# Batch 0's first product taken by halves of the contraction depth, with eight PSUM banks open at once

## The reference

```
y    = einsum('bsi,boi->bso', x, weight[ids])
base = einsum('bth,oh->bto', y, W_up)
z    = einsum('nh,erh->ner', y, lora_A);  logits = y @ gate_w.T + bias
out  = x + base + one_hot(argmax(logits)) applied to einsum('ner,ehr->neh', z, lora_B)
```

## Time and profile before

| | |
|---|---|
| median of 3 runs | 369.82 us (369.79 to 369.99) |
| the profiled execution's own time | 369.84 us |
| its span, first to last instruction | 368.1 us |
| busy: PE / PEld / DVE / ACT | 363.1 / 325.2 / 271.6 / 157.9 us |

### The profile page before, as it was taken

One profiled execution on the slowest core, in us unless ns is written; L12 is line 12 of the kernel. 1 busy time (PEld: TensorE's weight loads), 2 busy tenths in 40 slices (PEclk: granted clock), 3 DMA queues, 4 the chain that ended last, 5 costly groups with the idle time before them and its releaser, 6 DMA issues.

```text
span 368.1 us, 5953 instructions
## 1 busy us (share of the span) xinstructions
PE 363.1 (99%) x2193; PEld 325.2 (88%) x2193; DVE 271.6 (74%) x537; ACT 157.9 (43%) x315; POOL 1.8 (0%) x11
## 2 busy tenths in 40 slices
PE   7999999999999999999999999999999999999996
PEld 5888988899888998889988898888988899888995
DVE  4777847799478999678856788567984778856773
ACT  5677724645137533456025551155413553144300
POOL 0010000000000000000000000000000000000000
PEclk9999999999999999999999999999999999999999
DMA  7999984971079620686026750476404862160003
GB/s 246 396 401 307 405 318 174 325 251 51 0 274 330 223 89 2 250 319 232 0 116 234 267 187 2 170 264 211 157 0 180 325 213 85 49 238 0 3 0 114
DMA packets 20252, 68.16 MB, mean 185 GB/s; under 512 B 2304, under 2 KB 2688, under 8 KB 20224
## 3 DMA queue, kind: packets, MB, share of 16 engines
q1 hardware_dynamic: 19936, 66.74, 50.1%
q10 hardware_dynamic: 288, 1.05, 0.8%
HBM read 59.39 MB, written 8.39 MB: 184 GB/s over the span
## 4 chain that ended last, share of the span: by engine, by line
PE 99%; DVE 0%; issue 0%
PE ps_y L787 32%; PE ps_y L790 16%; PE ps_u L798 13%; PE ps_v L798 8%; PE ps_p L798 5%; PE ps_u L806 3%; PE ps_u L808 3%; PE ps_u L804 3%; PE ps_p L804 2%; PE ps_p L806 2%; PE ps_p L808 2%; PE ps_y L768 2%; PE ps_v L804 2%; PE ps_v L808 1%; PE ps_v L806 1%; PE ps_u L880 1%
## 5 line engine op out<-in xcount | busy, mean ns | idle before, releaser
L787 PE MATMUL ps_y<-x_hilo,w_hi 128*128 128x512 f32 x512 | 161.0, 396 | 0.0
L790 PEld LDWEIGHTS ps_y<-x_hilo,w_lo 128*128 128x128 f32 x512 | 96.2, 188 | 22.7
L790 PE MATMUL ps_y<-x_hilo,w_lo 128*128 128x256 f32 x512 | 100.6, 278 | 0.0
L506 DVE TENSOR_TENSOR w_lo<-w_raw,w_hi 128x512 fp32r<-128x512 f32 x126 | 81.6, 691 | 13.6 <-ACT w_hi L370 12.9
L787 PEld LDWEIGHTS ps_y<-x_hilo,w_hi 128*128 128x128 f32 x512 | 78.5, 189 | 0.9 <-DVE w_lo L499 0.4
L370 ACT CAST w_hi<-w_raw 128x512 fp32r<-128x512 f32 x126 | 71.8, 624 | 1.7 <-DMA w_raw<-w_dram 1.6
L385 ACT COPY small<-ps_y 128x256 f32<-128x256 f32 x64 | 23.9, 373 | 104.9 <-PE ps_y L790 104.9
L557 DVE TENSOR_TENSOR y_raw<-ps_y,small 128x256 f32<-128x256 f32 x64 | 27.1, 423 | 46.3 <-ACT small L385 46.3
L798 PE MATMUL ps_u<-wide_hi,y_parts 128*128 128x256 f32 (+1 forms) x256 | 47.2, 288 | 0.0
L798 PEld LDWEIGHTS ps_u<-wide_hi,y_parts 128*128 128x128 f32 x256 | 39.4, 188 | 1.4
L393 ACT CAST zT<-ps_y 128x128 fp32r<-128x128 f32 x16 | 3.5, 270 | 75.4 <-PE ps_y L814 75.4
(11 more groups left out here) (94 smaller groups left out, 386.0 us busy)
## 6 DMA issues: line engine op xcount, KB each, us to landing
w_raw<-w_dram SPq DMA_DIRECT2D x64, 512.0 KB, 4.7
rows<-x_dram SPq DMA_DIRECT2D x16, 512.0 KB, 5.9
out_dram<-rows SPq DMA_DIRECT2D x15, 512.0 KB, 2.7
x_raw<-xT_dram SPq DMA_DIRECT2D x14, 512.0 KB, 4.9
wide_raw<-w_up_dram SPq DMA_DIRECT2D x4, 512.0 KB, 11.2
thin_raw<-w_up_dram SPq DMA_DIRECT2D x4, 512.0 KB, 12.2
wide_stage<-w_up_dram SPq DMA_DIRECT2D x4, 512.0 KB, 13.9
thin_stage<-w_up_dram SPq DMA_DIRECT2D x4, 512.0 KB, 9.4
```

What stands on the lines that cost most here:

```text
L506: dve.tensor_tensor(w_lo[:, n % RAWS, part], w_raw[:, n % RAWS, part], w_hi[:, n % RING, part].bitcast(F32), ALU.subtract).then_inc(w_read ...
L787: pe.matmul(ps_y[c % 2][:, :], w_hi[:, n % RING, i * P:(i + 1) * P], x_hilo[:, :, i, :], start=(i == 0), stop=False)
L790: last = pe.matmul(ps_y[c % 2][:, S:2 * S], w_lo[:, n % RAWS, i * P:(i + 1) * P], x_hilo[:, 0, i, :], start=False, stop=(i == KC - 1))
```

## The change

Batch 0's first product becomes `open_product`: for the first half of the depth (steps 0 to 3) all 8 blocks are started, each in a PSUM bank of its own (`ps_open`: the six banks of ps_u, ps_v, ps_p and then the two of ps_y), and then all 8 are finished with the second half (steps 4 to 7). W of batch 0 comes in half blocks of 256 KB, two blocks' halves in one transfer (`load_pair`; pairs 0 to 3 hold the first halves, 4 to 7 the second halves), in runs of 2 KB; pair 0 is two transfers of 256 KB. x[0]'s second half is issued by SP between pairs 2 and 3. The warm-up has 11 matmuls. ACT and DVE split x's first half, pairs 0 to 3, x's second half, pairs 4 and 5, unit 0, pair 6 and unit 1 before the first evacuation; pair 7 follows the evacuation of block 0, unit 2 that of block 2.

```diff
-    WARM = 18
+    WARM = 11
     def splits_at(b, c):
+        if b == 0:
+            return (OC - 1,) if c == 0 else ()
-    UNIT_AT = {(0, 5): 0, (0, 6): 1, (0, 7): 2}
+    UNIT_AT = {(0, 2): 2}
+        ps_open = [ps[:, i, :] for ps in (ps_u, ps_v, ps_p) for i in range(2)] + [ps[:, :] for ps in ps_y]
+        def y_bank(b, c):
+            return ps_open[c] if b == 0 else ps_y[c % 2]
+        def wait_for_use(engine, n):
+            if n < OC // 2:
+                engine.wait_ge(half_done, n + 1)
+            elif n < OC:
+                engine.wait_ge(block_done, 2 * (n - OC // 2) + 2)
+            else:
+                engine.wait_ge(block_done, n + 1)
+            def load_pair(n, i):
+                if n >= RAWS:
+                    wait_for_use(sp, n - RAWS)
+                h, c = n // (OC // 2), 2 * n % OC
+                depth = slice(h * HK * P, (h + 1) * HK * P)
+                if n > 0:
+                    sp.dma_start(w_raw[:, n % RAWS, :].rearrange("p (a n) -> p a n", a=2),
+                                 w[bass.ds(i * OC + c, 2), :, depth].rearrange("a p n -> p a n")
+                                 ).then_inc(w_raw_in[n % RAWS], 16)
+                else:
+                    for a in range(2):
+                        sp.dma_start(w_raw[:, 0, a * HK * P:(a + 1) * HK * P],
+                                     w[bass.ds(i * OC + a, 1), :, depth].rearrange("a p n -> (a p) n")
+                                     ).then_inc(w_half_in if a == 0 else w_raw_in[0], 16)
             i = adapter(0)
-            i = load_blocks(0, 4, i)
+            for n in range(3):
+                load_pair(n, i)
+            sp.dma_start(x_raw[:, 1, XS:KC, :], xT[0, :, XS:KC, :]).then_inc(x_raw_in[1], 16)
+            load_pair(3, i)
             for n in range(4, OC):
                 load_unit(n - 4)
-                i = load_blocks(n, n + 1, i)
+                load_pair(n, i)
...
             def y_small(b, c):
                 act.wait_ge(block_done, b * OC + c + 1)
+                if b == 0 and c >= 2:
+                    act.wait_ge(y_full_ready, c - 1)
+                act.copy(small[:, c % 2, :], y_bank(b, c)[:, S:2 * S]).then_inc(y_small_ready, 1)
...
+            def open_product():
+                for h in range(HALVES):
+                    for c in range(OC):
+                        m = h * OC + c
+                        n = m // 2
+                        for k in range(h * HK, (h + 1) * HK, 2):
+                            if c == 0:
+                                pe.wait_ge(x_ready, k // XK + 1)
+                            if m > 0:
+                                pe.wait_ge(w_ready, 2 * (m + 1))
+                            else:
+                                pe.wait_ge(w_hi_ready, k // QK + 1)
+                            at = [(c % 2 * HK + i % HK) * P for i in (k, k + 1)]
+                            for i in range(2):
+                                pe.matmul(ps_open[c], w_hi[:, n % RING, at[i]:at[i] + P], x_hilo[:, :, k + i, :],
+                                          start=(k + i == 0), stop=False)
+                            if m == 0:
+                                pe.wait_ge(w_ready, k // QK + 1)
+                            for i in range(2):
+                                last = pe.matmul(ps_open[c][:, S:2 * S], w_lo[:, n % RAWS, at[i]:at[i] + P],
+                                                 x_hilo[:, 0, k + i, :], start=False, stop=(k + i == KC - 1))
+                        if h == 1:
+                            last.then_inc(block_done, 1)
+                        elif c % 2 == 1:
+                            last.then_inc(half_done, 1)
...
                 if b == 0:
                     pe.wait_ge(gl_ready, 2)
+                    pe.wait_ge(y_full_ready, 6)
```

More of the change, by code:

```diff
@@ L357, in x_hi, with first_w_hi @@
                 act.copy(x_hilo[:, 0, ks, :], x_raw[:, 1, ks, :]).then_inc(x_hi_ready, 1)
-            def first_w_hi(q):
+            def first_w_hi():
+                act.wait_ge(w_half_in, 16)
+                for q in range(2):
+                    part = slice(q * QK * P, (q + 1) * QK * P)
+                    act.copy(w_hi[:, 0, part], w_raw[:, 0, part]).then_inc(w_hi_ready, 1)
                 act.wait_ge(w_raw_in[0], 16)
-                part = slice(q * QK * P, (q + 1) * QK * P)
-                act.copy(w_hi[:, 0, part], w_raw[:, 0, part]).then_inc(w_hi_ready, 1)
+                part = slice(HK * P, KC * P)
+                act.copy(w_hi[:, 0, part], w_raw[:, 0, part]).then_inc(w_hi_ready, 2)
             def w_hi_part(n):
                 if n >= RING:
-                    act.wait_ge(block_done, n - RING + 1)
+                    wait_for_use(act, n - RING)
                 act.wait_ge(w_raw_in[n % RAWS], (n // RAWS + 1) * 16)
@@ L467, in strassen @@
                     w_hi_part(n)
[L469 to L472 removed]
+            act.dma_start(x_raw[:, 1, 0:XS, :], xT[0, :, 0:XS, :]).then_inc(x_raw_in[0], 16)
+            for q in range(XQ // XD):
                 x_hi(0, q)
[L474 to L480 removed]
+            first_w_hi()
+            for n in range(1, OC // 2):
+                w_hi_part(n)
+            for q in range(XQ // XD, XQ):
+                x_hi(0, q)
+            for n in (4, 5):
+                w_hi_part(n)
+            unit_hi(0)
+            w_hi_part(6)
+            unit_hi(1)
             for b in range(B):
@@ L494, in x_lo, with first_w_lo @@
                                   ALU.subtract).then_inc(x_ready, 1)
-            def first_w_lo(q):
-                dve.wait_ge(w_hi_ready, q + 1)
-                part = slice(q * QK * P, (q + 1) * QK * P)
-                dve.tensor_tensor(w_lo[:, 0, part], w_raw[:, 0, part], w_hi[:, 0, part].bitcast(F32),
-                                  ALU.subtract).then_inc(w_ready, 1)
+            def first_w_lo():
+                for first, stop, count in ((0, QK, 1), (QK, HK, 2), (HK, KC, 4)):
+                    dve.wait_ge(w_hi_ready, count)
+                    part = slice(first * P, stop * P)
+                    dve.tensor_tensor(w_lo[:, 0, part], w_raw[:, 0, part], w_hi[:, 0, part].bitcast(F32), ALU.subtract
+                                      ).then_inc(w_ready, 2 if first == HK else 1)
             def w_lo_part(n):
@@ L746, in _ @@
             dve.tensor_copy(warm[:, :], warm_f[:, :]).then_inc(warm_ready, 1)
-            for q in range(XQ - 1):
+            for q in range(XQ // XD):
                 x_lo(0, q)
-            for q in range(QUARTERS // 2):
-                first_w_lo(q)
-            x_lo(0, XQ - 1)
-            for q in range(QUARTERS // 2, QUARTERS):
-                first_w_lo(q)
-            for n in range(1, AHEAD):
-                w_lo_part(n)
+            first_w_lo()
+            for n in range(1, OC // 2):
+                w_lo_part(n)
+            for q in range(XQ // XD, XQ):
+                x_lo(0, q)
+            for n in (4, 5):
+                w_lo_part(n)
+            unit_lo(0)
+            w_lo_part(6)
+            unit_lo(1)
             for b in range(B):
```

29 lines of the change are left out of this document (10 added, 19 removed).

## The result

The changed kernel takes 372.43 us (median of 13 runs, 371.23 to 375.23); the kernel before took 369.90 beside it (13 runs, 369.64 to 370.36). The ratio is 1.0079 with an interval of 1.0061 to 1.0098: slower by 0.6 to 1.0%. The forecast of 370.3 is missed, and the time lies outside its range of 368.9 to 371.1. The profiled execution took 372.34, with a span of 370.6 and a mean granted clock of 1.00.

The account below looks back on a forecast made before the run. PE was taken to bound the kernel (99% of the chain). 1.55 at the start, less 0.7 of small waits and 1.29 of new wait, gave -0.43: 369.84 + 0.43 = 370.3 us, range 368.9 to 371.1.

Parts of the forecast that it names:

- The start: PE's first real matmul at 7.0 in place of 8.54, 1.55 earlier.
- The mechanism: At the product's end DVE's work behind the last W decides, not PE; PE waits 1.29 ahead of `plain(0)`.
- unit 3 is covered: Behind `plain(0)`'s start: unit 3 split by 33.5 against 36.1 wanted; without that cover each us late would be a us.
- the term for the landings of the loads: SP's queue: pair 1 lands at 9.3, pair 6 at 21.3 (bounds 21.0 and 22.4), pair 7 at 23.9.
- rival B: Late loads at the product's end: slower by more than 0.74; pair 6 at 22.4 gives 371.4; chance 0.19.
- a slow stretch: Loads at 8.3 to 9.8 before the change: it cost 0.5, of which 0.25 was expected back for pair 6.
- Rival D: Clock falls in the 1.3 wait or after the warm-up, costing about 2.2 in the second stage: 372.5; chance 0.02.
- Rival C: Paired transfers slow at 270 GB/s, 1.94 in place of 1.3 each: 4.5 us over seven pairs, 374.8; chance 0.03.
- Rival A: Loads come early and PE's own product end decides: 369.0, lower end 368.9; chance 0.20.
- Rival E: First W lands at 7.6 as before, start gains nothing, time unchanged; chance within the 0.56 shared with the main case.

Follow-up runs that it names:

- e6: Changed kernel with unit 2 split behind the first product and both gate pieces split ahead of A11's parts; 371.77 us.
- e5: Changed kernel reading pairs 1 to 7 from a second copy of W laid out by pairs, in 4 KB runs; 371.87 us.
- t1: e5 with pair 0 also loaded as one 512 KB transfer in 4 KB runs; 371.27 us.
- e1: Changed kernel with 13 warm-up matmuls in place of 11 and three more ahead of block 1's and block 2's first half; 373.29 us.
- e4: Changed kernel with x's second half issued on ACT's queue right behind the first half; 371.82 us.
- e9: Changed kernel with only the load order changed: pair 5 ahead of unit 0, pair 6 of unit 1, pair 7 of unit 2; 370.70 us.
- b1: Kernel before, with only W0 and W1 each cut into two transfers of 256 KB; 370.77 us.
- t3: t1 with the load order of e9; 369.21 us.
- t4: t3 with gate pieces ahead of A11's parts, and units 2 and 3 behind the first product, ahead of A12's parts; 368.60 us.
- b2: b1 with PE starting on the cast alone and 13 warm-up matmuls; 370.83 us.

## Why the prediction was wrong

Its steps, with what the profiled execution of the changed kernel shows:

| step | foretold | measured |
|---|---|---|
| PE's first real matmul | 7.0 | 7.11 |
| pair 0's second half lands | 7.1 | 8.1 |
| pair 0's second block | 8.63 | 9.68 |
| pair 1 lands | 9.3 | 10.5 |
| block 2 starts | 10.83 | 12.05 |
| product ends (14 x 1.39 more) | 30.35 | 31.5 |
| pair 6 lands | 21.3 | 23.1 |
| pair 7 lands | 23.9 | 26.1 |
| unit 1's subtraction starts | 23.55 | 25.30 |
| `plain(0)` starts | 31.64 | 33.55 |

**What held.** The start, within 0.1, and that by luck: the issue of W's first transfer had been put at 4.32 and its landing 2.13 later; it was issued at 3.96 and took 2.6. The mechanism held: DVE's work behind the last pairs decides, not PE. The chain from pair 6's landing to `plain(0)`, foretold as 10.34, measured 10.45, with 0.14 of it from pair 7; so DVE's paces and the order in which its pieces come were right. It held too that everything behind `plain(0)` only shifts, and that unit 3 is covered in the changed kernel (the cover is gone in e6).

**The step that failed** is the term for the landings of the loads, at both places. "I put its landing at 9.3" and "I take 21.3 (bounds by these corrections 21.0 with all the gains, and 22.4 with the worst runs alone)": pair 1 came 1.2 later, and pair 6 1.8 later, beyond that worst bound. This is rival B, to which the text gave 0.19. I had credited pair 6 with 0.55 for x out of the way and for half of a slow stretch, and then took off another 0.2 for being free of x, which counts x twice; the trace told nothing of how small transfers fill the engines. Of the 1.8, e5 accounts for 0.5: the form of the pairs cost 0.8 beside the changed kernel's profile (0.9 to 1.3 beside the other four of the same loads), where 0.3 had been taken, and 0.2 stood as an estimate from the Trainium skill ("DMA: Bandwidth & Descriptors", "Why small descriptors are slow"). Pair 0 as one whole transfer may bring another 0.3 (t1 against e5), which is no more than pair 6 differs between executions of the same loads (23.18 to 23.73). No run isolates the cause of the remainder, about 1.0; the 0.75 that was credited would be most of it, if none of it came. Carried through, 23.1 + 10.34 gives 33.44 for `plain(0)`, 0.11 short of the measured start, and 369.84 + 33.44 - 31.21 = 372.1, beside the 372.34 of the profiled execution.

The text counted from pair 6 alone and took pair 7 as "there". By its own sum pair 7 had some 0.3 to spare; it landed 3.0 behind pair 6 in place of 2.6, which used this up, and in e1 and e4, at 4.1 behind, it set the end by itself. So "Every us of pair 6 is a us of the end" holds only while pair 7 keeps its distance.

**Pair 1** set PE's own end as well. With 10.5 the product ends at 31.5 by the text's count, and its last matmuls start 0.56 later than those of the kernel before. So even with the late wait removed (e9) the change doesn't win: the early start of 1.43 is more than paid back, as the second half block and the third start 1.18 and 0.98 later than a dense product would have them, where the kernel before lost under 0.4 in all. That pair 1 is late because of the form of pair 0 is shown by t1 against e5 (8.94 against 10.63), and b1 shows the like in the kernel before. The text had treated the smaller transfer as a gain only: "at 392 GB/s 0.7, at W0's own pace 1.1".

**Rival D** had 0.02 and a price of 2.2. Its price was too high: e1 shows 1.3 for the fall. The runs with a clock of 0.995 lie 1.8 above the others by their medians, but that can hold a longer wait too. Its chance was far too low, 5 runs in 13. It depends on B, as later pairs make a longer wait. **Rival C** (paired reads far slower) is refuted: in 13 to 23, where pairs and units came by turns, the changed kernel moved 398 GB/s and e5, with 4 KB runs, 410. **Rival A's** floor was never reached; e9 removes the wait, but not the early ones. **Rival E** fell: the start did gain.

**Open.** Why the engines are a quarter idle in 5 to 8 with transfers of 256 KB and 2 KB runs, whether by their size or by their runs: no run changed one of these alone in pair 0. Also open are the varying distance from pair 6 to pair 7, and the early issue in t3 and t4. A near rival of the change itself was not run: the kernel before, with whole blocks, where PE starts on the cast alone. b2 did this only together with the small transfers.

## What to carry to other kernels

An early start on part of the data is worth only what the second and third pieces can keep up with: ask when the next transfers land, with the new sizes, before the gain is counted. When a chain hangs on a late load, follow the load behind it too, price the landings from both sides and let the range reach the time that the late side gives, since the chain itself (here 10.34 against 10.45) is the surer part. And a product that closes all its blocks at the end moves its evacuation behind the last load; the order of the queue (e9, 1.7 us for loads in another order) is then the first thing to alter.
